# The second mixer's k and v by seven block products in place of eight, on one Trainium2 core

## The reference, cut to what matters

```python
q = _phi(heads(x @ Wq + bq))      # _phi(t) = elu(t) + 1
k = _phi(heads(x @ Wk + bk))
v = heads(x @ Wv + bv)
kv = jnp.einsum('bhnd,bhne->bhde', k, v)
ksum = k.sum(axis=2)
z = 1.0 / jnp.einsum('bhld,bhd->bhl', q, ksum)
num = jnp.einsum('bhld,bhde->bhle', q, kv)
normed = num * z[..., None]
return out @ Wo + bo
```

## Time and profile before

| | us |
|---|---|
| median of 3 runs | 2670.67 |
| lowest, highest | 2668.65, 2671.88 |
| the profiled execution's own time | 2667.01 |
| its span, first to last instruction | 2665.3 |

### The profile page before, as it was taken

How to read it: one execution, slowest core, us unless ns; L and a number is a source line. 1 busy time by engine, 2 the same in 40 slices (tenths; PEclk the granted TensorE clock), 3 DMA queues, 4 the chain that set the end, 5 groups by cost and what they waited for, 6 DMA issues and landing times.

```text
span 2665.3 us, 26854 instructions
## 1 busy us (share of the span) xinstructions
PE 2586.9 (97%) x10727; PEld 1835.0 (69%) x10727; DVE 1546.5 (58%) x2637; ACT 780.0 (29%) x1314; POOL 347.5 (13%) x197
## 2 busy tenths in 40 slices
PE   7999999999999998999999999999999999999999
PEld 4667676658966987777777775555755786556676
DVE  4556461799947996988888997121342561341322
ACT  1043342017723763322222222420002331432000
POOL 0888888000000000000000000000000000000000
PEclk9999999999999998999999999999999999999999
DMA  8232313542020305000120004000350100212201
GB/s 253 29 40 13 49 5 46 146 145 75 20 59 12 104 19 194 1 1 1 71 101 1 24 24 172 11 0 36 79 161 18 36 1 1 69 69 84 86 24 58
DMA packets 137285, 155.70 MB, mean 58 GB/s; under 512 B 96508, under 2 KB 107606, under 8 KB 135634
## 3 DMA queue, kind: packets, MB, share of 16 engines
q1 hardware_dynamic: 66441, 153.56, 18.5%
q0 software_dynamic: 70720, 0.43, 2.7%
HBM read 117.75 MB, written 35.83 MB: 58 GB/s over the span
## 4 chain that ended last, share of the span: by engine, by line
PE 51%; DVE 7%; ACT 2%; DMA 1%; issue 1%; SPq 0%; DVEq 0%; ACTq 0%
PE psum L517 51%; DVE arena L1834 2%; DVE arena L1836 1%; DVE arena L1835 1%; DVE arena L1827 0%; ACT arena L1100 0%; ACT arena L1105 0%; ACT arena L991 0%; DVE arena L1492 0%; DVE arena L1900 0%; PE psum L528 0%; DVE arena L1334 0%; DVE arena L1833 0%; DVE arena L1826 0%; DVE arena L1859 0%
## 5 line engine op out<-in xcount | busy, mean ns | idle before, releaser
L517 PE MATMUL psum<-arena 128*125 128x384 f32 (+10 forms) x9816 | 2478.1, 414 | 39.3 <-DMA arena<-in_ffn_w 7.9
L517 PEld LDWEIGHTS psum<-arena 128*125 128x125 f32 (+3 forms) x9816 | 1733.3, 188 | 758.3 <-issue 135.7
L2161 POOL DMA_INDIRECT count_matrix<-arena x170 | 342.8, 2017 | 118.9 <-DVE arena L1431 59.4
L1834 DVE RECIPROCAL arena<-arena 128x500 f32<-128x500 f32 x60 | 196.7, 3278 | 2.1
L1584 DVE CUSTOM_DVE_ANT_0 arena<-arena 125x1250 bf16<-125x1250 bf16 (+1 forms) x100 | 139.2, 1457 | 12.9 <-ACT arena L1133 12.3
L2171 POOL MEMSET arena<- 125x60 f32 x1 | 0.2, 207 | 980.5 <-PE psum L517 980.5
L1668 DVE TENSOR_TENSOR arena<-arena 125x1250 f32<-125x1250 f32 x80 | 116.3, 1453 | 18.6 <-ACT arena L1082 18.3
L1079 ACT ACTIVATE arena<-arena 125x1250 f32<-125x1250 f32 x80 | 106.9, 1336 | 53.5 <-PE psum L517 53.2
L1671 DVE SCALAR_TENSOR_TENSOR arena<-arena 125x1250 f32<-125x1250 f32 x80 | 116.9, 1461 | 2.8
L991 ACT ACTIVATE arena<-psum 128x250 f32<-128x250 f32 (+1 forms) x102 | 40.8, 491 | 239.6 <-PE psum L528 239.2
L1225 ACT ACTIVATE arena<-psum,arena 128x250 f32<-128x250 f32 x120 | 49.2, 464 | 200.3 <-PE psum L517 200.3
(11 more groups left out here) (214 smaller groups left out, 1419.6 us busy)
## 6 DMA issues: line engine op xcount, KB each, us to landing
arena<-in_ffn_w SPq DMA_DIRECT2D x3, 4608.0 KB, 13.8
residual<-arena SPq DMA_DIRECT2D x30, 336.0 KB
arena<-residual SPq DMA_DIRECT2D x30, 336.0 KB
arena<-target_rows SPq DMA_DIRECT2D x12, 610.4 KB
arena<-in_gat_w SPq DMA_DIRECT2D x3, 2304.0 KB, 9.8
arena<-residual SPq DMA_DIRECT2D x10, 672.0 KB
residual<-arena SPq DMA_DIRECT2D x10, 672.0 KB
count_matrix<-arena SPq DMA_DIRECT2D x2, 3125.0 KB, 26.3
```

The source lines that it names most:

```text
L517: return pe.matmul(o, lhsT, rhs, start=start, stop=stop, skip_group_check=share)
L1834: now(dve.reciprocal(t_, t_))
L2161: pool.indirect_dma_start(counts[k], bass.IndirectOffsetOnAxis(ap=IDX_I[0:T, c:c + 1].bitcast(U32), axis=0), COUNT_I[0:T, c:c + 1], None, ...
```

## The change

For k (all five pairs of tiles) and for v (pairs 1 to 4; tiles 0 and 1 stay as they were) the product of a pair of tiles is cut into two by two blocks: two tiles by two halves of the contraction (features 0 to 383 and 384 to 767, three blocks each) on the left, two halves of the contraction by two halves of the columns on the right. Seven products of such blocks, of three matmuls each, and sums replace eight. Call them by the number in `product(...)`. PE issues 1, 5, 6, 3, 7, 2, 4. Products 1, 6, 7 and 4 share bank a, 5 and 3 bank b, and 2 has bank c; 6, 3, 7 and 4 add to what is in the bank, so that the bank holds a running sum that DVE reads between them into K1 or V1 and adds there.

DVE makes four sums of the input per pair (`x_sum`, 128x375 each, into XS, two buffers) and four sums of each weight (`weight_sums`, `last_weight_sum`, 128x1152 each; the last one overwrites a quarter of the weight). Those for k and for pair 0 stand between the second and third column group of q1, those of later pairs between the drains of the pair ahead, and those for v behind the last phi(k). The work on phi(k) (`elu`) is spread between the drains. ACT takes the four quarters of a pair in another order. TV, the sums of Wv, lies in WF[1], where Wo goes; Wo is therefore loaded behind the last v product. TK lies where V1 begins, and POOL writes V1's ones and clears KVB behind the last k product.

```diff
-    V.extend(("k1", t, half) for t in range(NT) for half in range(2))
-    V.extend(("v1", t, half) for t in range(NT) for half in range(2))
+    V.extend(("k1", p, i) for p in range(5) for i in "bca")
+    V.extend(("v1", t, half) for t in range(2) for half in range(2))
+    V.extend(("v1", p, i) for p in range(1, 5) for i in "bca")
...
+        XS = [mem(D_AT + KD * N + i * 1500, 4, 3, T) for i in range(2)]
+        assert D_AT + KD * N + 3000 <= F_AT
+        TK, TV = mem(B_AT, 3, 3, HALF), mem(F_AT + KD * D, 3, 3, HALF)
...
-            for t in range(NT):
-                for half in range(2):
-                    natural_product("V", ("k1", t, half), WF[1], HALF, XT, n0=half * HALF, tile=t)
+            def mixer_pair(name, p, weight, weight_sums, i, n):
+                low, high = slice(0, 3), slice(3, 6)
+                tile = [slice((2 * p + j) * T, (2 * p + j + 1) * T) for j in range(2)]
+                xs = XS[i % 2]
+                left = [XT[:, low, tile[0]], XT[:, high, tile[0]], xs[:, 3], XT[:, high, tile[1]], xs[:, 0], xs[:, 1], xs[:, 2]]
+                right = [weight[:, low, 0:HALF], weight[:, high, 0:HALF], weight[:, high, HALF:], weight_sums[:, 2],
+                         weight_sums[:, 0], weight_sums[:, 1], weight[:, low, HALF:]]
+                bank_b, bank_c, bank_a = (fill("V", (name, p, j)) for j in "bca")
+                def product(j, b, done, begin=False):
+                    for k in range(3):
+                        last = mm(b[0:T, 0:HALF], left[j - 1][:, k, :], right[j - 1][:, k, :], begin and k == 0, k == 2,
+                                  share=True)
+                    last.then_inc(done, 1)
+                product(1, bank_a, mixer_filled, True)
+                pe.wait_ge(x_sums, i + 1)
+                pe.wait_ge(wk_sums if name == "k1" else wv_sums, 1)
+                product(5, bank_b, mixer_filled, True)
+                pe.wait_ge(mixer_read, 4 * n + 1)
+                product(6, bank_a, mixer_filled)
+                pe.wait_ge(mixer_read, 4 * n + 2)
+                product(3, bank_b, v_filled)
+                pe.wait_ge(mixer_read, 4 * n + 3)
+                product(7, bank_a, mixer_filled)
+                product(2, bank_c, v_filled, True)
+                pe.wait_ge(mixer_read, 4 * n + 4)
+                product(4, bank_a, v_filled)
+            for p in range(5):
+                mixer_pair("k1", p, WF[1], TK, p, p)
             pe.wait_ge(m1w[2], 16)
-            for t in range(NT):
+            for t in range(2):
                 for half in range(2):
                     natural_product("V", ("v1", t, half), WF[0], HALF, XT, n0=half * HALF, tile=t)
+            for p in range(1, 5):
+                mixer_pair("v1", p, WF[0], TV, 4 + p, 4 + p)
             pe.wait_ge(te_used, 18 + 20)
             pe.wait_ge(kvb_zero, 2)
-            pe.wait_ge(v_drained, V_AT[("v1", NT - 1, 1)] + 1)
+            pe.wait_ge(v_drained, V_AT[("v1", 4, "a")] + 1)
...
-            for t in range(NT):
-                for half in range(2):
-                    act.wait_ge(v_drained, V_AT[("k1", t, half)] + 1)
+            for p in range(5):
+                for tt, half, bank_name in ((0, 1, "b"), (1, 1, None), (0, 0, "c"), (1, 0, "a")):
+                    t = 2 * p + tt
+                    if bank_name is None:
+                        act.wait_ge(mixer_read, 4 * p + 4)
+                    else:
+                        act.wait_ge(v_drained, V_AT[("k1", p, bank_name)] + 1)
...
-            n_te = 0
+            def weight_sums(w, o):
+                w11, w12, w21, w22 = (w[:, 3 * i:3 * i + 3, j * HALF:(j + 1) * HALF] for i in range(2) for j in range(2))
+                now(dve.tensor_tensor(o[:, 0], w12, w11, ALU.subtract))
+                now(dve.tensor_tensor(o[:, 1], w22, o[:, 0], ALU.subtract))
+                now(dve.tensor_tensor(o[:, 2], w21, o[:, 1], ALU.subtract))
+            def last_weight_sum(w, done):
+                dve.tensor_tensor(w[:, 0:3, HALF:], w[:, 3:6, HALF:], w[:, 0:3, HALF:], ALU.subtract).then_inc(done, 1)
+            x_tok = [0]
+            def x_sum(i, part):
+                p, o = (i if i < 5 else i - 4), XS[i % 2]
+                a11, a12, a21, a22 = (XT[:, 3 * k:3 * k + 3, (2 * p + j) * T:(2 * p + j + 1) * T] for j in range(2) for k in range(2))
+                after(x_tok[0])
+                if part == 0:
+                    x_tok[0] = step(dve.tensor_tensor(o[:, 0], a21, a22, ALU.add))
+                elif part == 1:
+                    x_tok[0] = step(dve.tensor_tensor(o[:, 1], o[:, 0], a11, ALU.subtract))
+                elif part == 2:
+                    x_tok[0] = step(dve.tensor_tensor(o[:, 2], a11, a21, ALU.subtract))
+                else:
+                    dve.tensor_tensor(o[:, 3], a12, o[:, 1], ALU.subtract).then_inc(x_sums, 1)
+            def elu(t, half):
+                cols = slice(half * HALF, (half + 1) * HALF)
+                dve.wait_ge(te_made, n_te[0] + 1)
+                k_ = K1[0:T, t, cols]
+                dve.scalar_tensor_tensor(k_, k_, 0.0, TE[n_te[0] % 2][0:T, 0:HALF], ALU.max, ALU.add).then_inc(te_used, 1)
+                n_te[0] += 1
+            def mixer_pair(name, p, n, o, bias, sums_of, elus):
+                bank_b, bank_c, bank_a = (bank((name, p, j)) for j in "bca")
+                shape = (lambda v: v) if name == "k1" else (lambda v: v.rearrange("p (a b) -> p a b", a=3))
+                def first(b, tt, h, done):
+                    dve.tensor_tensor(o(2 * p + tt, h), shape(b[0:T, 0:HALF]), shape(bias[0:T, h * HALF:(h + 1) * HALF]),
+                                      ALU.add).then_inc(done, 1)
+                def add(b, tt, h, done):
+                    dve.tensor_tensor(o(2 * p + tt, h), shape(b[0:T, 0:HALF]), o(2 * p + tt, h), ALU.add).then_inc(done, 1)
+                dve.wait_ge(mixer_filled, 4 * n + 1)
+                first(bank_a, 0, 0, mixer_read)
+                if sums_of is not None:
+                    x_sum(sums_of, 0)
+                dve.wait_ge(mixer_filled, 4 * n + 2)
+                first(bank_b, 1, 1, mixer_read)
+                if elus and p > 0:
+                    elu(2 * p - 2, 0)
+                dve.wait_ge(mixer_filled, 4 * n + 3)
+                first(bank_a, 0, 1, mixer_read)
+                if sums_of is not None:
+                    x_sum(sums_of, 1)
+                if elus and p > 0:
+                    elu(2 * p - 1, 0)
+                dve.wait_ge(v_filled, V_AT[(name, p, "b")] + 1)
+                dve.wait_ge(mixer_read, 4 * n + 3)
+                add(bank_b, 0, 1, v_drained)
+                if sums_of is not None:
+                    x_sum(sums_of, 2)
+                dve.wait_ge(mixer_filled, 4 * n + 4)
+                add(bank_a, 1, 1, mixer_read)
+                if sums_of is not None:
+                    x_sum(sums_of, 3)
+                if elus:
+                    elu(2 * p, 1)
+                dve.wait_ge(v_filled, V_AT[(name, p, "c")] + 1)
+                add(bank_c, 0, 0, v_drained)
+                if elus:
+                    elu(2 * p + 1, 1)
+                dve.wait_ge(v_filled, V_AT[(name, p, "a")] + 1)
+                first(bank_a, 1, 0, v_drained)
+            n_te = [0]
             for c, (n0, n) in enumerate(CH):
                 for m in range(KD):
-                    dve.wait_ge(te_made, n_te + 1)
-                    dve.tensor_tensor(QT1[:, m, n0:n0 + n], TE[n_te % 2][:, 0:n], TR[n_te % 2][:, 0:n],
+                    dve.wait_ge(te_made, n_te[0] + 1)
+                    dve.tensor_tensor(QT1[:, m, n0:n0 + n], TE[n_te[0] % 2][:, 0:n], TR[n_te[0] % 2][:, 0:n],
                                       ALU.add).then_inc(te_used, 1)
-                    n_te += 1
-            for t in range(NT):
-                for half in range(2):
-                    cols = slice(half * HALF, (half + 1) * HALF)
-                    dve.wait_ge(v_filled, V_AT[("k1", t, half)] + 1)
-                    b = bank(("k1", t, half))
-                    dve.tensor_tensor(K1[0:T, t, cols], b[0:T, 0:HALF], ROW[2][0:T, cols], ALU.add).then_inc(v_drained, 1)
-                    dve.wait_ge(v_drained, count[0])
-                    dve.wait_ge(te_made, n_te + 1)
-                    e_ = TE[n_te % 2][0:T, 0:HALF]
-                    k_ = K1[0:T, t, cols]
-                    dve.scalar_tensor_tensor(k_, k_, 0.0, e_, ALU.max, ALU.add).then_inc(te_used, 1)
-                    n_te += 1
-            for t in range(NT):
+                    n_te[0] += 1
+                if c == 1:
+                    dve.wait_ge(m1w[1], 16)
+                    dve.wait_ge(a_drained, A_AT[("tr", "ln1", 2, KD - 1)] + 1)
+                    weight_sums(WF[1], TK)
+                    last_weight_sum(WF[1], wk_sums)
+                    for part in range(4):
+                        x_sum(0, part)
+            for p in range(5):
```

(27 more changed lines are left out.)

## The result

The changed kernel takes 2650.82 us (median of 4 runs, 2650.61 to 2654.75), the one before beside it 2669.66 (4 runs, 2667.53 to 2671.88): ratio 0.9932, 95% interval 0.992 to 0.9944. Forecast were 2653.4 and faster. Run again (five executions, beside nine of the one before) it took 2649.93, ratio 0.9927 (0.9914 to 0.9941).

A forecast was written before the change was run, and what follows sets the result against it. PE was taken to bound the kernel: 27 matmuls x 0.645 = 17.42 us, less 0.1 of waiting, saves 17.3. From 2667.01 that gives 2649.7, and from the median, 3.66 higher, 2653.4; range 2649.5 to 2659.0.

The forecast's parts named there:

- The price of a matmul: In k and v, each matmul taken out saves its pitch of 0.645 us; 27 matmuls save 17.42 us.
- the step that the rows did not cover: In k and v, DVE's fullest slots hold 1.67 us of work against 1.935 per three-matmul product, so DVE keeps up.
- The cover: At hand-overs in k and v, DVE's read may be 1.38 us late before PE loses time.
- The sums ahead of k: Beside q1, DVE's weight and input sums take 7.7 us; margin 1.1 us, cost zero, or 1.0 at the upper bound.
- The wait for Wv's last sum: In v's first pair in blocks, product 5 waits up to 0.1 us for that sum, 0.4 as upper bound.
- Rival C: Within k pairs each elu waits for ACT, losing 0.96 us per slot, 19 us in all: 2672; chance 0.05.
- B: The sums block q1 longer than covered, up to the whole 7.7 us: 2661.1; chance 0.06.
- D: Short idles at k and v hand-overs halve PE's clock to 1.2 GHz; half the stage gives 2722; chance 0.02.
- E: Wo, wanted after n1, lands late, needing over 29 us: 2654 to 2660; chance 0.01.
- The size of the whole: Whole kernel: 17.3 us saved, 2649.7 for an execution like the profiled one; the median 3.66 higher, 2653.4.
- The range: Whole kernel: 2649.5 to 2659.0, from 2 us between medians, 1.0 + 0.3 for sums, up to 3 for B.

The follow-up runs named there:

- the sums made four times: Changed kernel with input sums of k's pairs 1 to 4 and v's pairs 2 to 4 made four times; q1's second group to kv1 took 188.93 us.
- phi(k) at once: Changed kernel with every phi(k) step of DVE directly behind its own quarter's drain; q1's second column group to kv1 took 184.25 us.

## Why the prediction was right

- **The price of a matmul.** 27 x 0.645 = 17.42. With the one wait removed the stretch gains 17.34, and k alone 9.66 of 9.68. That DVE's order does not cost PE anything, the step that the rows did not cover, holds: drains at the pitch of the products, PE full, clock 1.00.
- **The cover** is there, but it is 1.03 us and not 1.38. The prediction counted it up to the moment at which the product between ends; a read must be done some 0.3 us before that (the last section has the reason). In the changed kernel itself no read comes late. The expectation of the sums made four times, 4.8 us against 4.68 measured, agrees by luck: its slots were 0.1 to 0.2 us too long each (2.76 and 3.32 against 2.68 and 3.15), and that made up for a cover 0.34 too large. It also had the first k pair lose as much as the others, 0.8 to 0.95; it lost 0.46, like a v pair.
- **The sums ahead of k.** Reckoned at 7.7 us, they run from 1719.11 to 1726.77, 7.66. The margin of 1.1 us ahead of q1's last product is real, if a little smaller: 4.18 us more work cost 3.26, so 0.92 was free.
- **The wait for Wv's last sum** was priced too low, at up to 0.1 us (0.4 as the upper bound), and measured 0.31. The sum itself took 1.35 as reckoned and was done at 1816.95, 0.1 ahead of product 1's end. What failed is the step that took "done before the product ends" for "free of charge", the same one as in the cover.
- **Rival C** was priced wrongly, though not believed: it charged 0.96 us for each phi(k) that waits in the slot of its drain and forgot the cover named a few lines above it. Measured, all 20 cost nothing, the latest read (0.96 us) with little to spare under 1.03.
- **Rivals B, D and E** did not come. What would bring about B and E was made on purpose, and PE then stopped where they said. D asks for a clock that falls through short idles. Seven stops of 0.20 to 0.68 us within the stage, and one of 3.00 ahead of it, left the granted clock at 1.00. Only the 8.48 us behind the stage brought it to the lower level, and that cost 1.7 us (32.92 against 31.23) besides the gap. A stage that cycles through the lower level again and again, as D supposes, was not made.
- **The size of the whole.** An execution like the profiled one was put at 2649.7. The one that came to the stretch at the same time as that of before took 2649.93. The median was put at 2653.4 and came 2.6 lower: the step from one profiled execution to a median, 3.66 us above it, was the weak one, since executions differ by that much ahead of the stretch. Why before's median lies 3 us above its profiled execution and after's does not is open; with four to nine runs it may be chance.
- **The range** held with luck at its lower end. Its terms give 2 us below the forecast, 2651.4, and both medians (2650.82 and 2649.93) lie under that; no term leads to the 2649.5 that was written.

## What to carry to other kernels

Where one engine is full and clock and gaps say so, a matmul taken out is worth its pitch between starts, provided that every hand-over it brings has a product of other work between the read and its use. Check such a form by following how late each read becomes since DVE last waited for PE, and hold that against the cover; neither the fullest slot nor the sum over a period decides. Slots 2% over a product and a read 0.96 us late cost nothing, while reads 1.50 us late cost 0.47 each in pairs that kept DVE busy for 11.88 of 14.02 us. Where a one-time block of work goes beside another stage, count the buffers of that stage; the count here told both the margin and where PE would stop.

## What the runs showed that was not expected

A PE that stops pays more than its idle time. With the sums made four times the seven gaps add up to 2.8 us, but the stretch grew by 4.68: 0.26 to 0.27 more for each stop. One gap of 3.00 us cost 3.26, the same 0.26. And the wait for Wv's sum cost 0.31, where the rows show 0.07 us of idle time. The single records around one of the seven stops (four narrow windows of that trace) show what the rest is:

```profile
1752.66 0.81 PE L523 MATMUL psum<-arena 128*125 128x384 f32 x2
1754.13 0.18 PEld L523 LDWEIGHTS psum<-arena 128*125 128x125 f32 x1 [1.28 <-DVE arena L2023]
1754.13 0.59 PE L523 MATMUL psum<-arena 128*125 128x384 f32 x1 [0.67 <-DVE arena L2023]
1754.56 0.81 PE L523 MATMUL psum<-arena 128*125 128x384 f32 x2
```

In a full stream a record lasts 0.485 us but the next one starts after 0.322 (two take 0.81), so 0.16 of each lies over its successor. A gap is counted from the end of a record, and this 0.16 is lost unseen. In the stream a weight load starts together with the matmul ahead of its own; the one at the stop is itself held back by the drain and starts at 1754.13, together with its own matmul; that first record then lasts 0.59, and the next starts 0.42 behind it instead of 0.32. Together 0.67 + 0.16 + 0.10 = 0.93, which is the loss of that pair. At q1's last product the same terms give 3.00 + 0.16 + 0.10, and at Wv's sum 0.07 + 0.16 + 0.07. The ends of matmuls in the records are modelled; what a stop costs in all is read from starts alone.

So for these f32 matmuls a stop is priced at its gap plus 0.26. The read or sum that releases PE must be done 0.3 to 0.4 us before the recorded end of the matmul ahead: from the losses and the ends of the records it is 0.32 for the drains and 0.38 for Wv's sum, and a drain that was done 0.39 before cost nothing (phi(k) at once).
